# Causal attention and a gated FFN on one core: seven PSUM banks in one ring, exps per bank, and new orders of TensorE's work

## The chip, the cores and the metric

One core of a Trainium2 chip runs the kernel. The metric is device time in microseconds (us); the times before are three runs, and their median counts. Engines are called PE (TensorE), DVE (VectorE), ACT (ScalarE), POOL (GpSimd) and SP (SyncE, which only issues DMAs here).

## The reference

Eight batches `b` of 512 positions and 128 channels, 16 heads of width 8, then a gated FFN with a hidden width of 384; a LayerNorm (no gain, no bias) follows each.

```python
qkv = x @ w_qkv                                   # x (8, 512, 128), w_qkv (128, 384)
q, k, v = split(qkv, 3) -> (B, H=16, T=512, D=8)
att = einsum('bhtd,bhsd->bhts', q, k) / sqrt(D)
att = softmax(where(causal, att, -inf))
x = layernorm(x + einsum('bhts,bhsd->bhtd', att, v))
gate, up = x @ wg.T, x @ wu.T                     # int32 weights times 1/127
h = silu(gate) * up
x = layernorm(x + h @ wd.T)
```

All of it is float32.

## The kernel before, in words

**Groups.** The heads are worked on four at a time. A group `G` (0 to 31) is one quarter of the heads of one batch; a batch is four groups. q and k rows are split into a high and a low part (`parts`), written to DRAM scratch and read back in the layout that products need (`rows_of`, `read_rows`, `write_parts` on SP), two heads on each half of the rows: a head `hh` lies at row 64 * (hh % 2).

**Three passes over a group, at different times.**
1. *Maxima*, two groups ahead (`LAG = 2`): `maxima(M, k)` computes q against k with queries on the partitions, one PSUM bank for each k of 0 to 9 (`max_blocks`), two banks per call; DVE's `reduce_bank` takes minus the row maximum out of each block. Banks 0 to 3 hold 512 columns, the rest 384 + 128 or 256 + 256.
2. *Negated maxima*: POOL splits them in two parts (`split_negmax`); PE transposes them (`turn_negmax(m)`, one 128-column transpose); ACT copies them out of PSUM (`copy_negmax`, nm_T, L811); SP writes them into further rows of q (`load_negmax`, two DMAs of 8 KB, L347). `scores(m, 0)` waits for that with `pe.wait_ge(nm_loaded[G % 2], NM_LOADED * (G // 2 + 1))`.
3. *Scores and values*: `scores(G, s)` computes k against q with keys on the partitions, with the negated maximum as extra rows, into a pair of banks (slot `s`, 0 to 4); ACT's `exp_slot` applies exp to the pair at once (1024 columns, L803) into `pt`; POOL clears the part of the diagonal blocks above the diagonal (`clear_diagonal`, L1082); `values(V, piece)` multiplies with v for the group before (V = G - 1), in five pieces ("0a", "0b", "1", "2", "3": 256, 256, 384, 256, 128 columns; float32, which the trace shows as two matmuls for each), into bank 7, which stays outside of all rings. v carries a column of ones, so the row sums come along. Every two groups ACT copies the sum out (`copy_out`), PE transposes it (`turn_out`, four transposes) and DVE divides (`normalise`).

**PSUM.** Of eight banks, four form two pairs (`st_ps`) that scores, projections and x's transposes use in turn (`SCORE_TURNS`); three (`mx_ps`) are for maxima, negmax transposes and output transposes in turn (`MAXIMA_TURNS`). A turn waits until the turn that had its bank before has been read out (`pair_free`, `bank_free`).

**Order.** Every engine runs a list written out by hand. PE's is `group0` to `group3` (G % 4 of 1, 2, 3, 0). ACT's loop runs, for each group: exps of slots 0 and 1, `copy_negmax(G + 1)`, exps of slots 2 and 3, copies, slot 4. Projections for later batches: V and the turn of x in group0, Q and K in group1. `add_zeros(n)` adds n products of zeros to bank 7 and changes no value. `group0` before:

```python
scores(G, 0); scores(G, 1); later_values(V, "0a"); maxima(M, 0)
later_values(V, "1", "0b"); turn_negmax(G + 1); maxima(M, 2); scores(G, 2)
turn_out(half_of(G)); scores(G, 3); maxima(M, 4); later_values(V, "2", "3")
scores(G, 4); maxima(M, 6); project_v(b + 1); maxima(M, 8)
```

After the last group comes the FFN, batch by batch (`turn_x1`, `gate_up`, `down`), with both LayerNorms on DVE and POOL.

Of the kernel before, what the change touches and what calls it, by code (L numbers as in the profile page):

```python
# [40 lines left out]
SLOTS = 5  # L41
UNITS = 2 * SLOTS
# [40 lines left out]
def pieces_read(V, s):  # L83

    order = PIECE_ORDER[V % NG]
    return 1 + max(order.index(piece) for piece in (("0a", "0b"), ("0a", "0b"), ("1", "3"), ("1", "3"), ("2",))[s])


def score_turns():


    turns = [("X0",), ("QK",), ("VX", 0), ("Q", 1), ("K", 1), ("W", 0), ("W", 1)]
    for G in range(GROUPS):
        turns += [("S", G, s) for s in range(SLOTS - 1)]
        b, n = (G - 1) // NG, (G - 1) % NG
        if n == 1 and b + 2 < B:
            turns.append(("Q", b + 2))
        turns.append(("S", G, SLOTS - 1))
        if n == 0 and b + 1 < B:
            turns.append(("VX", b + 1))  # L100
        if n == 1 and b + 2 < B:
            turns.append(("K", b + 2))
    return turns


def maxima_turns():


    turns = []
    for G in range(-LAG, GROUPS + 1):  # L110
        n = (G - 1) % NG
        for k in range(MX):
            if G + LAG < GROUPS:
                turns.append(("M", G + LAG, k))
            if k == (1, 3, 3, 1)[n] and 0 <= G + 1 < GROUPS:
                turns.append(("N", G + 1))
            if k == (3, None, 5, None)[n] and G > 1:
                turns.append(("O", (G - 3) // 2))
    return turns + [("O", 2 * B - 1)]


SCORE_TURNS = score_turns()
MAXIMA_TURNS = maxima_turns()


def attention_ffn(nc, x, w_qkv, w_gate, w_up, w_down, out):
    ctx = ExitStack()
    with ctx:  # L128
# [7 lines left out]
        st_ps = [psum[:, 0:2, :], psum[:, 2:4, :]]  # L136
        mx_ps = [psum[:, 4, :], psum[:, 5, :], psum[:, 6, :]]
# [131 lines left out]
        def pair_of(*turn):  # L269
            return st_ps[SCORE_TURNS.index(turn) % 2]  # L270

        def pair_free(*turn):

            t = SCORE_TURNS.index(turn) - 2
            if t < 0:
                return []
            kind, *at = SCORE_TURNS[t]
            if kind == "X0":
                return [(xt_copied, 1)]
            if kind == "QK":  # L280
                return [(lo_made, 2)]
            if kind == "VX":
                return [(v_copied, at[0] + 1)] + ([(xt_copied, at[0] + 2)] if at[0] + 1 < B else [])
            if kind == "W":
                return [(wff_copied, 2 + at[0])]
            if kind == "S":
                return [(exp_done, SLOTS * at[0] + at[1] + 1)]
            return [(full_made, 2 * at[0] - (1 if kind == "Q" else 0))]

        def bank_of(*turn):  # L290
            return mx_ps[MAXIMA_TURNS.index(turn) % 3]

        def bank_free(*turn):

            t = MAXIMA_TURNS.index(turn) - 3
            if t < 0:
                return []
            kind, *at = MAXIMA_TURNS[t]
# [6 lines left out]
        def whole_batches(step):  # L305
            for b in range(B):
                step(b, b % 2, b == 0, b == B - 1)

        x1_ps = psum[:, 6, :]

        def y_ps(c):
            return psum[:, 4, :] if c < B - 1 else x1_ps

        last_pair = SCORE_TURNS.index(("S", GROUPS - 1, SLOTS - 2)) % 2
        ff_pairs = [(psum[:, 2 * p, :], psum[:, 2 * p + 1, :]) for p in (last_pair, 1 - last_pair)] + [(psum[:, 5, :], pv_ps)]
# [8 lines left out]
        def _(sp):  # L326
# [47 lines left out]
            for b in range(B):  # L374
                u = b % 2
                for n in range(NG):
                    if NG * b + n + 2 < GROUPS:
                        load_negmax(NG * b + n + 2)
                    if n == 0 and b < B - 1:
                        for g in (2, 3):  # L380
                            if b > 0:
                                sp.wait_ge(st_full, SLOTS * NG * b)
                            read_rows(b + 1, 1 - u, g)
# [11 lines left out]
                    if n == 3 and b + 2 < B:  # L395
                        sp.wait_ge(st_full, SLOTS * NG * b + SLOTS * 2)
                        for g in range(2):
                            read_rows(b + 2, u, g)
# [8 lines left out]
        def _(pe):  # L407
            def take_pair(*turn):
                for sem_, value in pair_free(*turn):
                    pe.wait_ge(sem_, value)  # L410
                return pair_of(*turn)

# [10 lines left out]
            def turn_x(b, dst):  # L423
                pe.wait_ge(x_in[b % 2], 16 * (b // 2) + 16)
                transposes4(dst, xa[b % 2][:].rearrange("p n c -> p (n c)")).then_inc(xt_made, 1)

            def project(b, n, dst):
                pe.wait_ge(xt_copied, b + 1)
                pe.matmul(dst, wqkv[:, C * n:C * n + C], xT[:], start=True, stop=True).then_inc((q_made, k_made)[n], 1)  # L429

            def project_q(b):
                if b < B:
                    project(b, 0, take_pair("Q", b)[:, 0, :])

            def project_k(b):
                if b < B:
                    project(b, 1, take_pair("K", b)[:, 0, :])

            def project_v(b):

                if b < B:
                    pair = take_pair("VX", b)
                    pe.wait_ge(xt_copied, b + 1)
                    for n in range(NB):
                        last = pe.matmul(pair[:, 0, C * n:C * n + C], xT[:, P * n:P * n + P], wqkv[:, 2 * C:3 * C],
                                         start=True, stop=True)
# [10 lines left out]
            def turn_out(hf):  # L457
                if hf is not None:
                    bank = take_bank("O", hf)
# [3 lines left out]
            def scores(G, s):  # L463
                u, g = G // NG % 2, G % NG
                if G < GROUPS:
                    if s == 0:
                        pe.wait_ge(nm_loaded[G % 2], NM_LOADED * (G // 2 + 1))
                    pair = take_pair("S", G, s)
                    for bank in (2 * s, 2 * s + 1):
                        blocks = [(hh, j) for hh in range(HG) for j in range(NB) if key_block_place(hh, j)[0] == bank]  # L470
                        for n, (hh, j) in enumerate(blocks):
                            col, width, at = key_block_place(hh, j)[1], T - P * j, 64 * (hh % 2)
                            last = pe.matmul(pair[:, bank % 2, col:col + width],  # L473
                                             kx[u][at:at + KS, 2 * g + hh // 2, P * j:P * j + P].bitcast(F32R),
                                             qx[u][at:at + KS, 2 * g + hh // 2, P * j:T].bitcast(F32R),
                                             start=(n == 0), stop=(n == len(blocks) - 1), skip_group_check=True)
                    last.then_inc(st_full, 1)

            def maxima(M, k):

                if M < GROUPS:
                    u, g = M // NG % 2, M % NG
                    if k == 0:
                        pe.wait_ge(qk_loaded[u][g], LOADED * (M // NG // 2 + 1))
                    for k in (k, k + 1):
# [50 lines left out]
            def group0(G):  # L536
                V, M, b = G - 1, G + LAG, G // NG
                scores(G, 0)
                scores(G, 1)
                later_values(V, "0a")  # L540
                maxima(M, 0)
                later_values(V, "1", "0b")
                if V == 0:
                    add_zeros(4)
                turn_negmax(G + 1)
                maxima(M, 2)
                scores(G, 2)
                turn_out(half_of(G))
                scores(G, 3)
                maxima(M, 4)  # L550
                later_values(V, "2", "3")
                scores(G, 4)
                maxima(M, 6)
                if b + 1 == B:
                    add_zeros(4)
                project_v(b + 1)
                maxima(M, 8)

            def group1(G):
                V, M, b = G - 1, G + LAG, G // NG  # L560
                values(V, "0a")
                scores(G, 0)
                scores(G, 1)
                maxima(M, 0)
                values(V, "1", "0b")
                maxima(M, 2)
                turn_negmax(G + 1)
                scores(G, 2)
                values(V, "2")
                maxima(M, 4)  # L570
                scores(G, 3)
                if b + 2 == B:
                    maxima(M, 6)
                    add_zeros(4)
                    scores(G, 4)
                    maxima(M, 8)
                    add_zeros(3)
                    values(V, "3")
                else:
                    values(V, "3")  # L580
                    maxima(M, 6)
                    project_q(b + 2)
                    scores(G, 4)
                    maxima(M, 8)
                    project_k(b + 2)

            def group2(G):
                V, M = G - 1, G + LAG
                maxima(M, 0)
                scores(G, 0)  # L590
                values(V, "0a")
# [611 lines left out]
```

## Time and profile before

| | |
|---|---|
| median of 3 runs | 353.14 us (351.8 to 357.61) |
| profiled execution, its own time | 353.12 us |
| its span | 351.4 us |
| PE busy | 333.8 us, 95% |
| DVE busy | 294.0 us, 84% |
| ACT busy | 214.7 us, 61% |
| POOL busy | 178.4 us, 51% |

The span is the time between the first and last record in the trace; the time has a little around it. Busy time counts an instruction from its start to its end, so overlapping matmuls on PE count once and a PE that is waiting with one in flight is busy. PEld is the loading of weights, which runs beside the matmuls.

### The profile page before, as it was taken

To read this page: it belongs to the slowest core of one execution; us is meant where nothing else is said; L and a number is where in the kernel's file an instruction comes from. 1 tells how busy PE (TensorE), PEld (TensorE's weight loads), DVE (VectorE), ACT (ScalarE), POOL (GpSimd) and SP (SyncE) were. 2 spreads that over 40 slices of the span, in tenths; PEclk is the share of its full clock that TensorE was granted. 3 is DMA by queue.
4 is the path that set the end of the run, shared out by engine and by line. 5 is a ranking of instruction groups with operands and counts; after the bars stand their busy time and mean duration, and the time that the engine had idled before them with its cause. 6 is when DMAs were issued, how large, how long until landed. Compare 5 with 4: busy or idle time off the path is not lost. (4 is left out here: it accounts for less than half of the span.)

```text
span 351.4 us, 9106 instructions
## 1 busy us (share of the span) xinstructions
PE 333.8 (95%) x2947; PEld 197.1 (56%) x2947; DVE 294.0 (84%) x1251; ACT 214.7 (61%) x277; POOL 178.4 (51%) x325
## 2 busy tenths in 40 slices
PE   7799999999999999999999999999999998999990
PEld 3444464556556555645564565456455544798980
DVE  7979778898899889889898998899898974867765
ACT  3402567777767768677777777776677784333320
POOL 8400334734654474357445534843434469787633
PEclk9999989999999999999999999999999999999997
DMA  5797242554265327624541653185100010002021
GB/s 155 288 296 250 62 123 64 197 171 123 62 245 174 109 73 261 168 73 169 198 121 34 245 147 110 41 288 165 49 2 5 5 34 1 3 30 62 30 62 60
DMA packets 33903, 41.75 MB, mean 119 GB/s; under 512 B 3136, under 2 KB 17472, under 8 KB 33856
## 3 DMA queue, kind: packets, MB, share of 16 engines
q1 hardware_dynamic: 33696, 40.91, 36.7%
q8 instruction: 24, 0.39, 0.5%
q10 hardware_dynamic: 160, 0.26, 0.2%
q14 instruction: 23, 0.19, 0.2%
HBM read 21.76 MB, written 18.87 MB: 116 GB/s over the span
## 5 line engine op out<-in xcount | busy, mean ns | idle before, releaser
L903 DVE CUSTOM_DVE_ANT_0 masked<-psum,mask 128x384 bf16<-128x384 f32 (+3 forms) x512 | 218.9, 487 | 30.7 <-PE psum L490 26.5
L803 ACT ACTIVATE pt<-psum 128x1024 f32<-128x1024 f32 x160 | 158.4, 1021 | 51.8 <-PE psum L473 51.2
L1082 POOL TENSOR_SCALAR_AFFINE_SELECT pt<-pt 128x512 f32<-128x512 f32 x128 | 79.6, 634 | 95.7 <-ACT pt L803 93.9
L490 PE MATMUL psum<-kx,qx 33*128 33x384 f32 (+3 forms) x512 | 91.8, 354 | 1.6 <-DVE nm L903 0.7
L513 PE MATMUL psum<-pt,vx 128*32 128x256 f32 (+2 forms) x1280 | 92.1, 388 | 1.1 <-ACT oT L817 0.8
L473 PE MATMUL psum<-qx,kx 35*128 35x384 f32 (+3 forms) x512 | 75.4, 342 | 0.5 <-ACT pt L803 0.5
L490 PEld LDWEIGHTS psum<-kx,qx 33*128 33x128 f32 x512 | 53.2, 186 | 37.8 <-DVE nm L903 18.6
L473 PEld LDWEIGHTS psum<-qx,kx 35*128 35x128 f32 x512 | 45.7, 185 | 29.0 <-issue 15.1
L513 PEld LDWEIGHTS psum<-pt,vx 128*32 128x32 f32 x1280 | 30.3, 109 | 38.3 <-issue 23.6
L903 DVE DVE_READ_ACCUMULATOR2_ANT nm<- 128x1 f32 x512 | 42.6, 83 | 0.0
L1070 POOL TENSOR_SCALAR nm_parts<-nm 128x16 fp32r<-128x16 f32 x32 | 6.6, 206 | 51.3 <-DVE nm L903 50.3
L867 ACT ACTIVATE sg<-psum 128x512 f32<-128x512 f32 x24 | 14.3, 598 | 27.6 <-PE psum L710 22.8
L811 ACT ACTIVATE nm_T<-psum 32x128 f32<-32x128 f32 x32 | 8.5, 266 | 26.1 <-PE psum L455 26.1
L723 PE MATMUL psum<-wT,pt 128*128 128x128 f32 x192 | 22.6, 275 | 0.0
L723 PEld LDWEIGHTS psum<-wT,pt 128*128 128x128 f32 x192 | 22.1, 192 | 0.1
L710 PE MATMUL psum<-x_lo,wT 128*128 128x512 f32 x48 | 19.2, 400 | 2.4 <-DVE x_lo L981 2.4
L708 PE MATMUL psum<-x_hi,wT 128*128 128x512 f32 x48 | 19.9, 415 | 0.0
L522 PE MATMUL psum<-zeros 128*128 128x512 bf16 x68 | 18.7, 406 | 1.2 <-DVE zeros L938 1.2
L993 DVE TENSOR_TENSOR pt<-psum,sg 128x512 f32<-128x512 f32 x24 | 15.8, 680 | 4.3 <-ACT sg L867 3.5
L429 PE MATMUL psum<-xT,wqkv 128*128 128x512 f32 x32 | 17.4, 636 | 0.1
L1101 POOL TENSOR_TENSOR parts<-full,parts 128x512 fp32r<-128x512 f32 x12 | 15.4, 1284 | 1.0
L1129 POOL TENSOR_TENSOR rstd<-veps,minus_half 128x4 f32<-128x4 f32 (+1 forms) x12 | 14.7, 1224 | 0.0
(64 smaller groups left out, 273.6 us busy)
## 6 DMA issues: line engine op xcount, KB each, us to landing
scr_q<-parts SPq DMA_DIRECT2D x16, 512.0 KB, 3.6
scr_k<-parts SPq DMA_DIRECT2D x16, 512.0 KB, 5.0
qx<-scr_q SPq DMA_DIRECT2D x64, 128.0 KB, 2.6
kx<-scr_k SPq DMA_DIRECT2D x62, 128.0 KB, 2.7
xa<-L_attn_x SPq DMA_DIRECT2D x8, 256.0 KB, 3.2
res<-L_attn_x SPq DMA_DIRECT2D x8, 256.0 KB, 2.8
out<-yo SPq DMA_DIRECT2D x8, 256.0 KB, 2.3
qx<-nm_T SPq DMA_DIRECT2D x64, 8.0 KB
```

Of the source, the lines that this page charges most:

```text
L429: pe.matmul(dst, wqkv[:, C * n:C * n + C], xT[:], start=True, stop=True).then_inc((q_made, k_made)[n], 1)
L473: last = pe.matmul(pair[:, bank % 2, col:col + width], kx[u][at:at + KS, 2 * g + hh // 2, P * j:P * j + P].bitcast(F32R), qx[u][at:at + KS ...
L490: last = pe.matmul(bank[:, col:col + width], qx[u][at:at + KM, 2 * g + hh // 2, P * i:P * i + P].bitcast(F32R), kx[u][at:at + KM, 2 * g + ...
L513: last = pe.matmul(pv_ps[VW * hh:VW * hh + VW, first:last_q], vx[u][:, at:at + VW], pt[g % 2][:, bank, col + first - P * j:col + last_q - ...
L522: pe.matmul(pv_ps, zeros[:, 0:P], zeros[:], start=True, stop=True, skip_group_check=True)
L708: pe.matmul(ff_ps(c, m)[n], w, x1_hi[c % 2][:].bitcast(F32R), start=True, stop=False)
L710: pe.matmul(ff_ps(c, m)[n], w, x1_lo[c % 2][:].bitcast(F32R), start=False, stop=True).then_inc(full, 1)
L723: last = pe.matmul(y_ps(c)[:, C * n:C * n + C], hid[c % 2][:, m, P * n:P * n + P], wT[:, 2, P * m:P * m + P], start=(m == 0 and n == 0), s ...
L803: act.activation(pt[G % 2][:, 2 * s:2 * s + 2, :], pair_of("S", G, s), ACT.Exp, scale=SM_SCALE).then_inc(exp_done, 1)
L903: dve.tensor_tensor_reduce(masked[count % 4][:, 0:width], bank[:, col:col + width], mask[:, T - width:T], -1.0, 3.0e38, ALU.add, ALU.min, ...
L993: dve.tensor_tensor(hid[c % 2][:, m, :], ff_ps(c, m)[1], sg[k % 2][:], ALU.mult).then_inc(hid_made, 1)
L1082: pool.affine_select(out=blocks, in_=blocks, pattern=[[0, HG], [1, P]], compare_op=ALU.is_ge, fill=0.0, base=0, channel_multiplier=-1).the ...
```

## The change

1. Both rings become one, `BANK_TURNS`, over seven banks (`RING = 7`): each turn, of whatever kind, takes the next bank and waits for the turn seven before it to be read out. The turn of x and the V projection, which shared a pair, are turns of their own.
2. Scores and exps go by banks: `scores(G, n)` for n of 0 to 9, and ACT's `exps` with 512 columns each instead of 1024.
3. `group0` to `group3` get new orders, with single banks of scores and maxima interleaved, and `turn_negmax` at other places; ACT's list puts `copy_negmax(G + 1)` behind exp 9 in group0 and group1, behind exp 3 in group2 and behind exp 8 in group3. DVE's `normalise` stands at other places.
4. Zero products: `project_v` adds four in the last batch, where there is nothing to project. Those of the first group (four) and of group1 in the batch before the last (four and three) go.
5. The FFN's banks get their numbers from the ring; `turn_out(2 * B - 1)` waits for the last exp.

```diff
-PIECE_ORDER = (("0a", "1", "0b", "2", "3"), ("0a", "1", "0b", "2", "3"), ("0a", "0b", "2", "3", "1"), ("0a", "0b", "1", "2", "3"))
+PIECE_ORDER = (("0a", "1", "0b", "3", "2"), ("0a", "1", "0b", "3", "2"), ("0a", "3", "2", "0b", "1"), ("0a", "0b", "1", "3", "2"))
...
+GROUP_TURNS = (
+    "s0 s1 m0 s2 s3 m1 m2 s4 m3 s5 m4 o n s6 m5 m6 s7 s8 s9 m7 m8 v x m9",
+    "m0 s0 s1 s2 s3 s4 m1 s5 m2 m3 m4 m5 s6 s7 m6 q s8 s9 m7 m8 n k m9",
+    "s0 s1 m0 m1 s2 m2 s3 n o s4 m3 s5 m4 m5 s6 m6 s7 m7 s8 m8 s9 m9",
+    "s0 s1 m0 s2 m1 s3 m2 s4 m3 s5 m4 n s6 m5 s7 s8 m6 m7 s9 m8 m9",
+)
...
+BANK_TURNS = bank_turns()
+RING = 7
...
+        def bank_of(*turn):
+            return psum[:, BANK_TURNS.index(turn) % RING, :]
+
+        def bank_free(*turn):
+
+            t = BANK_TURNS.index(turn) - RING
             if t < 0:
                 return []
...
+            if kind == "V":
+                return [(v_copied, at[0] + 1)]
             if kind == "W":
+                return [(wff_copied, at[0] + 1)]
             if kind == "S":
+                return [(exp_done, UNITS * at[0] + at[1] + 1)]
...
                     last.then_inc(v_made, 1)
-                    if b + 1 < B:
-                        turn_x(b + 1, pair[:, 1, :])
+                else:
+                    add_zeros(4)
...
             def group0(G):
                 V, M, b = G - 1, G + LAG, G // NG
+                scores(G, 0, 1)
                 maxima(M, 0)
+                later_values(V, "0a", "1")
+                scores(G, 2, 3)
+                maxima(M, 1, 2)
+                scores(G, 4)
+                maxima(M, 3)
+                later_values(V, "0b")
+                scores(G, 5)
+                maxima(M, 4)
+                turn_out(half_of(G))
                 turn_negmax(G + 1)
+                scores(G, 6)
+                maxima(M, 5, 6)
+                scores(G, 7)
+                later_values(V, "3", "2")
+                scores(G, 8, 9)
+                maxima(M, 7, 8)
                 project_v(b + 1)
+                turn_x(b + 2)
+                maxima(M, 9)
...
             def group1(G):
...
                 maxima(M, 0)
+                scores(G, 0, 1, 2, 3)
+                values(V, "0a", "1")
+                scores(G, 4)
+                maxima(M, 1)
+                scores(G, 5)
+                maxima(M, 2, 3, 4)
+                values(V, "0b", "3", "2")
+                maxima(M, 5)
+                scores(G, 6, 7)
+                maxima(M, 6)
+                project_q(b + 2)
+                scores(G, 8, 9)
+                maxima(M, 7, 8)
                 turn_negmax(G + 1)
+                project_k(b + 2)
+                maxima(M, 9)
...
             def group2(G):
...
+                scores(G, 0, 1)
+                maxima(M, 0, 1)
+                scores(G, 2)
+                values(V, "0a", "3")
                 maxima(M, 2)
+                scores(G, 3)
                 turn_negmax(G + 1)
                 turn_out(half_of(G))
+                scores(G, 4)
+                maxima(M, 3)
+                scores(G, 5)
+                maxima(M, 4, 5)
+                scores(G, 6)
+                values(V, "2")
                 maxima(M, 6)
+                scores(G, 7)
+                maxima(M, 7)
+                scores(G, 8)
+                values(V, "0b", "1")
                 maxima(M, 8)
+                scores(G, 9)
+                maxima(M, 9)
...
             def group3(G):
                 V, M = G - 1, G + LAG
                 scores(G, 0)
+                values(V, "0a")
+                scores(G, 1)
                 maxima(M, 0)
+                scores(G, 2)
+                maxima(M, 1)
+                values(V, "0b")
+                scores(G, 3)
                 maxima(M, 2)
+                scores(G, 4)
+                maxima(M, 3)
+                scores(G, 5)
                 maxima(M, 4)
                 values(V, "1")
+                turn_negmax(G + 1)
+                scores(G, 6)
+                maxima(M, 5)
+                scores(G, 7, 8)
+                maxima(M, 6, 7)
+                values(V, "3", "2")
+                scores(G, 9)
+                maxima(M, 8, 9)
...
-            turn_out(2 * B - 1)
+            pe.wait_ge(exp_done, UNITS * GROUPS)
+            turn_out(2 * B - 1, last_out)
...
+            def exps(G, *banks):
+                for n in banks:
+                    act.wait_ge(st_full, UNITS * G + n + 1)
                     if G > 1:
+                        act.wait_ge(pv_piece, PIECES * (G - 2) + pieces_read(G - 2, n))
+                    act.activation(pt[G % 2][:, n, :], bank_of("S", G, n), ACT.Exp, scale=SM_SCALE).then_inc(exp_done, 1)
...
+            for G in range(1, GROUPS - 1):
                 b, n = (G - 1) // NG, (G - 1) % NG
+                if n == 0:
+                    exps(G, 0, 1, 2, 3, 4, 5, 6, 7, 8, 9)
+                    copy_negmax(G + 1)
+                    copy_v_and_x(b + 1)
+                elif n == 1:
+                    exps(G, 0, 1, 2, 3, 4, 5, 6, 7)
+                    copy_q_or_k(b + 2, 0)
+                    exps(G, 8, 9)
+                    copy_negmax(G + 1)
                     copy_out((G - 2) // 2)
+                    copy_q_or_k(b + 2, 1)
+                elif n == 2:
+                    exps(G, 0, 1, 2, 3)
+                    copy_negmax(G + 1)
+                    exps(G, 4, 5, 6, 7, 8, 9)
+                else:
+                    exps(G, 0, 1, 2, 3, 4, 5, 6, 7, 8)
+                    copy_negmax(G + 1)
                     copy_out((G - 2) // 2)
+                    exps(G, 9)
...
-                    if k == (3, None, 5, None)[(G - 1) % NG] and half_of(G) is not None and G < GROUPS - 1:
+                    if k == (4, None, 2, None)[(G - 1) % NG] and half_of(G) is not None and G < GROUPS - 1:
                         normalise(half_of(G))
...
-                    pool.wait_ge(exp_done, SLOTS * G + s + 1)
+                    pool.wait_ge(exp_done, UNITS * G + (4, 8, 10, 8)[j])
```

## Rows read from the trace of the kernel before

**Rows 1.** The page, busy time of each engine.

```profile
PE 333.8 (95%) x2947; PEld 197.1 (56%) x2947; DVE 294.0 (84%) x1251; ACT 214.7 (61%) x277; POOL 178.4 (51%) x325
```

**Rows 2.** The waits: engine, line and tile, releaser, total us, times, longest.

```profile
PEld psum L490 <- DVE nm L903: 18.6, 59, 0.5
...
PEld psum L473 <- ACT pt L803: 12.1, 23, 0.8
...
PEld psum L473 <- DMA qx<-nm_T: 0.4, 1, 0.4
```

**Rows 3.** Busy time by stretch: PE, PEld, DVE, ACT, POOL, clock, DMA.

```profile
154.15:186.67 32.52, 32.35 (x318) 17.76 (x316) 28.79 (x133) 24.02 (x31) 16.56 (x29) 1.00 0.46 148
```

**Rows 4.** Timeline of PE: start us, us, line, tiles, shapes, count.

```profile
150.66 0.50 PE L490 MATMUL psum<-kx,qx 33*128 33x512 f32 x2
151.09 0.33 PE L455 MATMUL psum<-identf,nm_parts 128*128 128x128 f32 x1
151.35 0.50 PE L473 MATMUL psum<-qx,kx 35*128 35x384 f32 x4
151.78 0.64 PE L513 MATMUL psum<-pt,vx 128*32 128x256 f32 x8
152.35 0.65 PE L490 MATMUL psum<-kx,qx 33*128 33x384 f32 x3
...
154.15 1.13 PE L429 MATMUL psum<-xT,wqkv 128*128 128x512 f32 x2
155.20 0.51 PE L473 MATMUL psum<-qx,kx 35*128 35x256 f32 x4
...
163.65 0.51 PE L473 MATMUL psum<-qx,kx 35*128 35x256 f32 x4
...
165.91 0.42 PE L513 MATMUL psum<-pt,vx 128*32 128x256 f32 x4
...
177.85 0.51 PE L473 MATMUL psum<-qx,kx 35*128 35x256 f32 x4
...
178.53 1.16 PE L445 MATMUL psum<-wqkv,xT 128*128 128x128 f32 x8
179.52 0.60 PE L420 MATMUL psum<-identf,xa 128*128 128x128 f32 x4
180.05 0.51 PE L490 MATMUL psum<-kx,qx 33*128 33x256 f32 x4
```

**Rows 5.** Timeline of all engines around two negmax loads.

```profile
29.26 0.27 ACT L811 ACTIVATE nm_T<-psum 32x128 f32<-32x128 f32 x1 [13.52 <-PE psum L455]
...
29.55 1.52 SPq L347 DMA_DIRECT2D qx<-nm_T  x2
...
32.41 0.19 PEld L473 LDWEIGHTS psum<-qx,kx 35*128 35x128 f32 x2 [0.42 <-DMA qx<-nm_T]
...
160.07 0.33 PE L455 MATMUL psum<-identf,nm_parts 128*128 128x128 f32 x1
...
160.44 0.27 ACT L811 ACTIVATE nm_T<-psum 32x128 f32<-32x128 f32 x1 [0.24 <-PE psum L455]
...
160.73 1.27 SPq L347 DMA_DIRECT2D qx<-nm_T  x2
```

**Rows 6.** Timeline of ACT: 1024 columns twice, and 512 columns twice.

```profile
160.61 1.90 ACT L803 ACTIVATE pt<-psum 128x1024 f32<-128x1024 f32 x2
...
212.17 0.60 ACT L789 ACTIVATE vx<-psum 128x512 f32<-128x512 f32 x1 [0.29 <-PE psum L445]
212.67 0.59 ACT L770 ACTIVATE xT<-psum 128x512 f32<-128x512 f32 x1
```

**Rows 7.** Busy time by stretch, columns as in rows 3.

```profile
46.00:47.00 1.00, 0.55 (x6) 0.56 (x8) 1.00 (x5) 1.00 (x2) 0.00 (x0) 0.87 0.06 16
47.00:50.00 3.00, 3.00 (x18) 2.73 (x14) 1.81 (x12) 1.69 (x3) 1.81 (x3) 0.50 0.91 248
...
290.00:292.00 2.00, 1.24 (x17) 0.44 (x9) 1.74 (x10) 1.42 (x2) 2.00 (x5) 1.00 0.00 0
```

More of the change, by code:

```diff
@@ L89, in score_turns @@
[L89 to L103, printed above, removed]
@@ L106, in maxima_turns, with bank_turns @@
[L106 to L115, printed above, removed]
+    return 1 + max(order.index(piece) for piece in (("0a", "0b") if n < HG else ("1", "3") if n < 2 * HG else ("2",)))
+GROUP_TURNS = (
[4 rows of a table added]
+)
+def bank_turns():
+    turns = [("X", 0), ("Q", 0), ("K", 0), ("V", 0), ("X", 1), ("Q", 1), ("K", 1), ("W", 0), ("W", 1), ("W", 2)]
+    turns += [("M", 0, k) for k in range(MX)]
+    turns += [("M", 1, 0), ("M", 1, 1), ("M", 1, 2), ("M", 1, 3), ("N", 0)] + [("M", 1, k) for k in range(4, 8)]
+    turns += [("S", 0, 0), ("S", 0, 1), ("M", 1, 8), ("M", 1, 9), ("S", 0, 2), ("S", 0, 3), ("M", 2, 0), ("M", 2, 1), ("N", 1)]
+    turns += [("S", 0, 4), ("S", 0, 5), ("M", 2, 2), ("M", 2, 3), ("S", 0, 6), ("S", 0, 7), ("M", 2, 4), ("M", 2, 5)]
+    turns += [("S", 0, 8), ("S", 0, 9)] + [("M", 2, k) for k in range(6, 10)]
+    for G in range(1, GROUPS - 1):
+        b = (G - 1) // NG
+        for turn in GROUP_TURNS[(G - 1) % NG].split():
+            if turn[0] == "s":
+                turns.append(("S", G, int(turn[1])))
+            elif turn[0] == "m" and G + LAG < GROUPS:
+                turns.append(("M", G + LAG, int(turn[1])))
+            elif turn == "n":
@@ L116, in maxima_turns @@
                 turns.append(("N", G + 1))
-            if k == (3, None, 5, None)[n] and G > 1:
+            elif turn == "o" and G > 1:
                 turns.append(("O", (G - 3) // 2))
-    return turns + [("O", 2 * B - 1)]
-SCORE_TURNS = score_turns()
-MAXIMA_TURNS = maxima_turns()
+            elif turn in ("q", "k") and b + 2 < B:
+                turns.append((turn.upper(), b + 2))
+            elif turn == "v" and b + 1 < B:
+                turns.append(("V", b + 1))
+            elif turn == "x" and b + 2 < B:
+                turns.append(("X", b + 2))
@@ L126, in attention_ffn @@
+    G = GROUPS - 1
+    return turns + [("S", G, n) for n in range(8)] + [("X1",), ("S", G, 8), ("S", G, 9), ("O", 2 * B - 2)]
+BANK_TURNS = bank_turns()
+RING = 7
 def attention_ffn(nc, x, w_qkv, w_gate, w_up, w_down, out):
@@ L455, in turn_negmax, with turn_out, scores @@
                     pe.transpose(bank[:, 0:P], nm_parts[:], identf[:]).then_inc(nm_turned, 1)
-            def turn_out(hf):
+            def turn_out(hf, bank=None):
                 if hf is not None:
-                    bank = take_bank("O", hf)
+                    if bank is None:
+                        bank = take_bank("O", hf)
                     pe.wait_ge(ot_copied, hf + 1)
                     transposes4(bank, oT[:]).then_inc(o_turned, 1)
-            def scores(G, s):
+            def scores(G, *banks):
@@ L566, in group1 @@
-                maxima(M, 2)
-                turn_negmax(G + 1)
[L568 to L585, printed above, removed]
+                scores(G, 0, 1, 2, 3)
@@ L867, in silu @@
                 act.activation(sg[k % 2][:], ff_ps(c, m)[0], ACT.Silu, scale=W_SCALE).then_inc(silu_done, 1)
-            for s in range(SLOTS - 1):
-                exp_slot(GROUPS - 1, s)
-            exp_slot(GROUPS - 1, SLOTS - 1)
+            exps(GROUPS - 1, 0, 1, 2, 3, 4, 5, 6, 7, 8, 9)
             copy_x1(0)
```

283 lines of the change are left out of this document (100 added, 183 removed).

## The prediction

> **What bounds the kernel now.** Five views, in this order, the last two at the parts that need them. The profile's page gives TensorE (PE) 95% of the span and VectorE (DVE) 84% [rows 1], so PE is read first; but a busy PE is not a full one, because matmuls in flight count as busy. The chain of waits shows what PE's weight loads stood behind: DVE's readings of the maxima banks 18.6 us, ScalarE's (ACT's) exps 12.1 us, and the load of the negated maxima once, 0.4 us [rows 2]. A stretch of one batch (from one Q projection to the next, four groups) lasts 32.52 us, with DVE busy 28.79 and ACT 24.02 [rows 3]. The third view is PE's timeline, read from start to start [rows 4]. There, work falls into runs of one kind, and every change of kind costs something:
> - scores and maxima together: one step (two banks, one on each half of the rows, side by side) 150.66 to 151.09, 0.43 us; two steps 177.85 to 178.53, 0.68. So 0.25 a step and 0.18 for the change of kind.
> - values: 256 columns 151.78 to 152.35, 0.57; I split that as 0.13 for the change and 0.44 for the work, 0.22 per 128 columns.
> - transposes: one 151.09 to 151.35, 0.26; four 179.52 to 180.05, 0.53.
> - projections: Q or K 154.15 to 155.20, 1.05; V 178.53 to 179.52, 0.99.
>
> The loops have per batch 20 runs with 40 steps (20 x 0.18 + 40 x 0.25 = 13.6 us), 14 runs of values (14 x 0.13 + 4 x 2.2 = 10.6), 7 of transposes (2.7) and 3.1 of projections: 30.0 of 32.5 us. The other 2.5 us are stalls; the largest is plain: 163.65 to 165.91 is 2.26 us for four steps that need 1.18 [rows 4]. PE bounds the kernel; DVE, busy for 28.79, is the next, 3.7 us behind it.
>
> **Part 1, fewer changes of kind (a gain).** I counted the new orders. A batch has 17 runs of scores and maxima (saves 3 x 0.18), 12 of values (2 x 0.13) and the negmax and output transposes in one run twice (2 x 0.13): 1.1 us. Bank n of scores and bank k of maxima lie on the row half of their parity, and all single turns find a partner of the other half, so 40 steps remain; the singles cost nothing. PE's floor is 28.9 us a batch.
>
> **Part 2, one ring of seven.** The most that it can return is all stalls, 2.5 us a batch; the least is below nothing, since a score bank now also waits for DVE and a maxima bank for ACT. Taken with part 3, where a wait that is longer swallows both.
>
> **Part 3, the negated maxima come later (the loss).** Scores of group G+1 start only when three steps behind `turn_negmax(G+1)` are done: ACT's `copy_negmax`, two DMAs on SP, their landing. The one place in the trace where PE waited for the landing prices it: copy started at 29.26, PE's weight load at 32.41 after 0.42 us idle, 3.15 us. SP's two issues take 1.27 us in the steady part (160.73) and took 1.52 there, so I take 2.9 us from copy start to scores; the ends are 2.6 and 3.15. From transpose to copy it is 160.07 to 160.44, 0.37 us [rows 5]. Before, the transpose stands early in every group and ACT copies after two exp slots, so this is covered. The new orders take the cover away at three of four borders:
> - group1 to group2: the transpose is near the end. Behind it PE has K's projection, 1.05, and at most 0.2. Needed: 0.37 + 2.9 = 3.3. PE stands at least 1.9 us, whatever ACT does. ACT is later still: it copies after exps 8 and 9. Scores 8 and 9 come 5.85 us after the group's first (runs 0.67, 1.2, 0.9, 1.2, 0.76, 1.05); their data 0.4 later; Q's copy and two exps at 0.50 each (212.17 to 212.67 for 512 columns [rows 6]) put the copy at about 7.4, the next scores at 10.3.
> - group0 to group1: ACT copies only after exp 9. First scores to scores 8: 5.8 us (0.5, 1.2, 0.9, 0.57, 0.43, 0.7, 0.67, 0.79); data and two exps 1.4; copy at 7.2; next scores at 10.1. In the ring, maxima 7 takes the negmax bank of the same group, so part of that wait shows already there.
> - group3 to group0: ACT copies after exp 8. Scores 8 comes 4.4 us in (0.43, 0.57, 0.68, 0.57, 0.93, 0.79, 0.26, 0.2); with exps 6 to 8 in a row the copy starts at 6.2, the next scores at 9.1. PE has 1.7 us of work behind scores 8 and needs 3.9 or more.
> - group2 to group3: the transpose is early. PE's work is 6.4 us (0.8, 0.8, 0.43, 0.7, 0.9, 0.57, 0.68, 1.2, 0.3); DVE's share of a group is 7.2 (28.79 / 4), of which the ring lets some spill into the next, so 6.6.
>
> Sum: 10.1 + 10.3 + 6.6 + 9.1 = 36.1 us a batch, against 32.5: +3.6. In seven batches 25 us, the two borders of the last batch 3.5 more (2.4 and 1.2, the second shorter since no maxima are left), less 2.6 for eleven zero products that go (seven in the batch before the last, four in the first group), each priced as a step of 512 columns: +26 us.
>
> Who stands behind the waits: on PE everything, since its order is fixed, so DVE runs dry after at most three or four reductions, and ACT and POOL with it. On SP the load is issued ahead of `read_rows` and `write_parts` as before; these shift with it and are needed a group or more later, so I charge nothing for them. If that cover were gone, a group's maxima would wait for rows, some 2.6 us a time.
>
> **Part 4, exps per bank.** Two of 1024 columns take 1.90 us together, one of 512 takes 0.50 to the next [rows 6]: 4.6 us a group become 5.0, 1.6 us a batch on an engine with 8.5 us free. It starts PE's bank turns sooner, and sits on the chain above only with its last one to three exps. POOL's diagonal clearing waits for the same data as before: nothing. The last stage, behind group 31, gets other bank numbers for the same products in the same order, with one more wait, for the last exp, ahead of the last `turn_out`; the projections of the gate and up weights cover it: nothing.
>
> **Part 5, the clock.** PE's granted clock fell once in mid-kernel: PE was busy for 0.55 of the microsecond 46 to 47, with scores and maxima alone (clock 0.87), then ran at 0.50, which is 1.2 of 2.4 GHz, in 47 to 50 [rows 7]. That is 0.26 + 3.0 us at half speed at the least, and half of it is lost: 1.6 us a fall. In 290 to 292 PE was busy for only 1.24 of 2 us beside dense products, and the clock held. The new stalls are of 1.9 to 2.3 us, between runs of scores. Some will make it fall; I take 9 of 23 borders, 1.6 us each, 14 us; the ends are none and 23 (37 us). The Trainium skill, page "TensorE: Matmul & The Clock Gate", section "A second HAM failure mode: psum-queue depth-cycling", says that a TensorE that idles briefly between groups of matmuls, while it cycles through PSUM banks, can swing between the two levels. Taken as a rule for every border it would give the upper end; the stretch at 290 us does not bear that out.
>
> **The sum.** Profiled before: span 351.4, time 353.12, equal to the median 353.14. 353 + 26 + 14 = 393 us.
>
> **The rivals.**
> 1. The waits bind and the clock holds throughout: 353 + 26 = 379 us; with 2.6 us for the load it is 7 less (0.3 at 22 borders), 372. For it: 290 to 292. Against: the fall in 46 to 47 us after far less idling.
> 2. The waits bind and the clock falls at most borders: 353 + 26 + 37 = 416. For it: that fall. Against: the stall of 163.65 to 165.91, also among scores and maxima, and no fall.
> 3. Faster: the load isn't late. Then the stalls of part 2 go and PE comes near its floor, with DVE (28.79 busy) as next bound: 29.8 us a batch would be 353 - 7.25 x 2.7 = 333 (2.7 is 32.5 less 29.8). It decides if copy to scores takes under about 0.8 us instead of 2.9 (6.3 us a batch less, over three borders). For it: only 0.4 us of waiting on that load in the trace [rows 2]. Against: 160.73 plus 1.27 of issuing alone is 1.56 us behind the copy's start [rows 5].
> 4. It changes nothing: the load is late, but the late transposes gain what they lose because PE would have stood for DVE anyway. At most the 2.5 us of stalls a batch and the 1.1 of part 1 can pay; that takes 1.2 us less at each of the three borders, a load of 1.7 us. About 353.
>
> **How the numbers follow.** Forecast (some falls) 0.46, rival 1 0.27, rival 2 0.10, rival 3 0.10, rival 4 0.07. Predicted 393. The range leaves out rivals 3 and 4 and the far end of 2: 364 (rival 1 with a load of 2.6, less 8 for what the runs of PE overlap better than priced) to 422 (rival 2 with a load of 3.15). A measurement here tells about 2% from no change, 7 us. Faster 0.10, same 0.07, slower 0.83.
>
> **What the profile after would show.** Right: PE or its weight loads waiting for the load of the negated maxima some 22 times, 1 to 2.3 us each, where it was 0.4 us in all; batches of some 36 to 38 us; DVE under 80%; several slices with a clock below 0.9; fewer changes of kind. Wrong if: those waits are short, since ACT or the DMAs are quicker than priced; or PE waits for DVE or ACT in the ring instead; or DVE is above 90% (rival 3). Forecast and rivals 1 and 2 are told apart by the granted clock alone.

## The result: 501 us, and the profile after

The changed kernel takes 500.95 us (median of 4 runs, 493.7 to 506.1) against 353.45 us: 1.40 times as long (95% interval 1.393 to 1.416). The ratio and its interval compare only runs within 1.5% of the fastest of their kernel, while the medians, here and below, are of all runs. The forecast was 393 us with a range of 364 to 422. The direction and the late load of the negated maxima were right; the price put on a fall of the clock was not, and the size was not even near.

The profiled execution's page, with its span, the busy times that answer to [rows 1], and the slices (busy tenths in 40 equal slices of the span, and PE's granted clock in tenths):

```profile
span 491.9 us, 9391 instructions
PE 442.4 (90%) x2936; PEld 255.6 (52%) x2936; DVE 297.4 (60%) x1251; ACT 225.9 (46%) x437; POOL 179.0 (36%) x325
...
PE   8898899998889999889889999889987988889993
...
PEclk9999955585755555585755555765557655799998
```

DVE does the same work as before (297.4 us, 294.0 before) in a span 140 us longer, so it is no bound. PE's busy time rose from 333.8 to 442.4 us with eleven matmuls fewer. Only the clock row explains that: from the sixth slice to the 34th it reads mostly 5, which is 1.2 GHz of 2.4. The mean over the span is 0.684; if every microsecond was at one of the two levels, 63% of the span was at the lower.

The chain of waits, with the rows that answer to [rows 2]:

```profile
PEld psum L464 <- DMA qx<-nm_T: 26.9, 16, 2.7
...
PE psum L464 <- DMA qx<-nm_T: 21.0, 14, 2.5
...
PEld psum L464 <- DVE nm L902: 20.2, 29, 1.5
...
PEld psum L480 <- ACT nm_T L807: 12.5, 8, 1.6
...
PEld psum L464 <- ACT pt L800: 11.2, 17, 0.8
```

The load of the negated maxima, 0.4 us in all before, now holds PE 16 times for 26.9 us; and eight times a maxima bank waits for ACT's copy of them, which is maxima 7 of group0 taking the negmax bank of its own group. The order of the wait can be read at one border, group1 to group2 (timeline of all engines):

```profile
163.42 0.47 PE L446 MATMUL psum<-identf,nm_parts 128*128 128x128 f32 x1
163.69 1.92 PE L420 MATMUL psum<-xT,wqkv 128*128 128x512 f32 x2
164.06 0.25 ACT L807 ACTIVATE nm_T<-psum 32x128 f32<-32x128 f32 x1
164.34 1.28 SPq L340 DMA_DIRECT2D qx<-nm_T  x2
166.97 0.29 PEld L464 LDWEIGHTS psum<-qx,kx 35*128 35x128 f32 x2 [0.93 <-DMA qx<-nm_T]
```

From copy to scores: 164.06 to 166.97, 2.91 us, where 2.9 was taken. The transpose stands last in the group, as the diff has it. But PE waits for only 0.93 us here, not for 1.9 or more, because K's projection behind the transpose runs at half speed. At a border that PE reaches at the full clock it stands longer: 2.17 us ahead of the scores at 61.56 us. Busy time by stretch (PE, PEld, DVE, ACT, POOL, clock, DMA), as in [rows 3] and [rows 7]:

```profile
48.00:51.00 3.00, 3.00 (x17) 2.61 (x14) 1.47 (x8) 0.60 (x1) 0.34 (x1) 0.50 0.39 103
51.00:61.00 10.00, 8.39 (x79) 4.51 (x79) 7.62 (x36) 7.40 (x15) 3.42 (x9) 0.99 0.27 78
61.00:102.00 41.00, 38.26 (x236) 21.59 (x237) 21.88 (x96) 17.73 (x35) 12.01 (x20) 0.51 0.29 97
102.00:112.00 10.00, 8.84 (x82) 4.66 (x80) 7.62 (x36) 7.75 (x16) 4.25 (x8) 0.98 0.30 88
...
133.00:208.00 75.00, 68.87 (x403) 38.36 (x403) 37.66 (x168) 32.12 (x63) 20.20 (x36) 0.50 0.26 81
```

The first fall, at 48 us, lasts 3 us, like the one in the kernel before. The next lasts 41 us, a later one 75. In all there are nine such stretches behind the first: 41, 13, 75, 14, 75, 44, 14, 24 and 3 us, some 304 us together. Eight of them begin beside a wait for the load, the last beside a wait of 2.20 us for one of ACT's copies. Matmuls pass at 8 a microsecond at the full clock (79 in 10 us) and 5.4 at the lower (403 in 75). One batch inside such a stretch, from V projection to V projection, takes 57 us against 32.5; V's projection itself 1.87 us (148.28 to 150.15) against 0.99 [rows 4]:

```profile
148.45:205.49 57.04, 53.95 (x317) 29.31 (x318) 29.56 (x133) 25.82 (x50) 16.63 (x29) 0.50 0.27 85
```

```profile
148.28 2.08 PE L436 MATMUL psum<-wqkv,xT 128*128 128x128 f32 x8
150.15 1.06 PE L408 MATMUL psum<-identf,xa 128*128 128x128 f32 x4
```

What stood ahead of the rises is mixed. The clock came back at the end of V's projection and x's transposes near 51, 102, 208 and 314 us, and behind values near 126, 232 and 389. It did not come back behind the V projection and transposes shown here, nor behind those at 254 us.

### The profile page after: what moved, and what is told of

Read it like the earlier page. It is cut to its first block and busy times, and to the rows that moved or that the text cites. A ratio compares the mean times of both kernels' runs of the same rounds, so it can differ in the third digit from the quotient of the medians.

```text
span 491.9 us, 9391 instructions
## 1 busy us (share of the span) xinstructions
PE 442.4 (90%) x2936; PEld 255.6 (52%) x2936; DVE 297.4 (60%) x1251; ACT 225.9 (46%) x437; POOL 179.0 (36%) x325
## 5 line engine op out<-in xcount | busy, mean ns | idle before, releaser
L800 ACT ACTIVATE pt<-psum 128x512 f32<-128x512 f32 x320 | 172.6, 598 | 172.8 <-PE psum L464 171.3
L464 PE MATMUL psum<-qx,kx 35*128 35x384 f32 (+3 forms) x512 | 145.6, 473 | 23.1 <-DMA qx<-nm_T 21.0
L480 PE MATMUL psum<-kx,qx 33*128 33x384 f32 (+3 forms) x512 | 145.6, 459 | 10.4 <-ACT nm_T L807 10.2
L503 PE MATMUL psum<-pt,vx 128*32 128x256 f32 (+2 forms) x1280 | 137.0, 558 | 2.7 <-ACT oT L813 2.2
L464 PEld LDWEIGHTS psum<-qx,kx 35*128 35x128 f32 x512 | 92.0, 271 | 89.0 <-DMA qx<-nm_T 26.9
L480 PEld LDWEIGHTS psum<-kx,qx 33*128 33x128 f32 x512 | 95.2, 268 | 48.1 <-issue 30.0
L503 PEld LDWEIGHTS psum<-pt,vx 128*32 128x32 f32 x1280 | 40.0, 140 | 49.8 <-issue 41.7
L420 PE MATMUL psum<-xT,wqkv 128*128 128x512 f32 x32 | 21.1, 757 | 0.0
L408 PE MATMUL psum<-identf,oT 128*128 128x128 f32 x64 | 16.4, 407 | 0.0
L436 PE MATMUL psum<-wqkv,xT 128*128 128x128 f32 x64 | 15.6, 420 | 0.0
```

The source lines that it names most:

```text
L408: last = pe.transpose(dst[:, P * n:P * n + P], src[:, P * n:P * n + P], identf[:])
L420: pe.matmul(bank, wqkv[:, C * n:C * n + C], xT[:], start=True, stop=True).then_inc((q_made, k_made)[n], 1)
L464: last = pe.matmul(bank[:, col:col + width], kx[u][at:at + KS, 2 * g + hh // 2, P * j:P * j + P].bitcast(F32R), qx[u][at:at + KS, 2 * g + ...
L480: last = pe.matmul(bank[:, col:col + width], qx[u][at:at + KM, 2 * g + hh // 2, P * i:P * i + P].bitcast(F32R), kx[u][at:at + KM, 2 * g + ...
L503: last = pe.matmul(pv_ps[VW * hh:VW * hh + VW, first:last_q], vx[u][:, at:at + VW], pt[g % 2][:, bank, col + first - P * j:col + last_q - ...
L800: act.activation(pt[G % 2][:, n, :], bank_of("S", G, n), ACT.Exp, scale=SM_SCALE).then_inc(exp_done, 1)
```

## The experiments

Two theories stood. Mine: the late negated maxima make PE stand at three of four borders, and standing lets the clock fall. The rival: the ring, the single exps or the new orders cost by themselves, in waits or through the clock.

### 1. The change with the negmax early

The ring, the exps of 512 and all orders stay; only the transpose and the copy move forward. In the ring's lists, in PE's functions and in ACT's loop alike:

```diff
-    "... m3 s5 m4 o n s6 ..."           # group0, ACT copies behind exp 9
+    "... m3 n s5 m4 o s6 ..."           # behind exp 4
-    "... m4 m5 ... s8 s9 m7 m8 n k m9"  # group1, behind exp 9
+    "... m4 n m5 ... s8 s9 m7 m8 k m9"  # behind exp 5
-                values(V, "1")          # group3, behind exp 8
                 turn_negmax(G + 1)
+                values(V, "1")          # behind exp 4
```

> The changed kernel with its ring, exps and orders, but the negmax transpose and ACT's copy of it early in every group (transposes ahead of scores 5 in group0, behind the values in the middle of group1, ahead of values 1 in group3; the copy behind exps 4, 5, 3 and 4). My theory (late negated maxima make PE stand at the group borders, and the standing keeps the clock down): waits for the negmax load under 3 us in all, clock over 0.95, DVE over 85% busy, 330 to 350 us. Rival (the ring and the new orders cost by themselves): waits for that load gone but the time over 370 us, with PE waiting for DVE or ACT at banks of the ring.

Measured: 344.32 us (340.1 to 348.8), 0.963 of the kernel before (0.955 to 0.971), mean clock 0.952. One batch, and the waits for the load:

```profile
137.83:167.75 29.92, 29.92 (x320) 17.82 (x316) 28.14 (x134) 24.85 (x51) 16.52 (x30) 1.00 0.50 162
```

```profile
PEld psum L464 <- DMA qx<-nm_T: 2.0, 2, 1.2
```

The rival falls: with everything else of the change in place, a batch takes 29.92 us against 32.52 [rows 3], and the whole kernel is faster than before. Moving one 128-column transpose and one copy, in three groups of every four, is worth 157 us. What still holds this version back shows behind the place where group1 of the batch before the last has no projections any more:

```profile
229.00:233.60 4.60, 4.60 (x57) 2.47 (x55) 3.63 (x15) 3.65 (x7) 2.73 (x5) 1.00 0.49 148
233.60:237.90 4.30, 3.29 (x28) 2.33 (x32) 4.30 (x27) 3.41 (x8) 1.81 (x3) 1.00 0.22 65
237.90:248.00 10.10, 10.10 (x73) 5.78 (x65) 6.22 (x28) 4.53 (x10) 2.28 (x5) 0.51 0.01 2
```

PE was busy for 3.29 of 4.30 us, with scores and maxima alone and DVE as the bound. Then the clock was at 0.51 for 10 us, though PE was never idle in them.

### 2. The kernel before with the negmax late

Pairs, three banks, exps of 1024 and the old orders; only the transpose and the copy move back to where the change has them, as near as pairs allow (in group3 the copy stands behind the last exp and not one ahead of it).

```diff
-            if k == (1, 3, 3, 1)[n] and 0 <= G + 1 < GROUPS:
+            if k == ((1, 3, 3, 1) if G < 1 else (5, 9, 3, 5))[n] and 0 <= G + 1 < GROUPS:
...
                 exp_slot(G, 1)
-                copy_negmax(G + 1)
+                if n == 2 or G < 1:
+                    copy_negmax(G + 1)
...
                 exp_slot(G, 4)
+                if n != 2 and G > 0:
+                    copy_negmax(G + 1)
```

(and `turn_negmax` in `group0`, `group1` and `group3` to match)

> The kernel before with its pairs, its three banks and its exps of 1024, but the negmax transpose and copy where the change has them (transpose behind maxima 4 in group0, behind the last maxima in group1, behind values 1 in group3; the copy behind the last exps there). My theory: the late load alone makes it slow, 430 to 510 us, with over 30 us of waits for the load and a mean clock of 0.65 to 0.8. Rival (the ring and orders do it): under 375 us, clock over 0.95.

Measured: 450.18 us (442.8 to 459.6), mean clock 0.831, waits for the load 40.4 us in 21 places:

```profile
PEld psum L473 <- DMA qx<-nm_T: 40.4, 21, 2.7
```

```profile
139.05:185.70 46.65, 42.17 (x318) 22.42 (x318) 29.22 (x133) 23.78 (x31) 16.61 (x29) 0.76 0.32 104
```

So the late load is also enough by itself, with no ring: 96 us between the medians, 91 between the fastest runs (442.8 and 351.7). The clock is down for less of the time than forecast (0.831, and 0.805 to 0.843 over the four runs; I expected at most 0.8).

### 3. The change, with zero products in place of idling

```diff
                     bank = take_bank("S", G, n)
                     if n == 0:
+                        for _ in range((0, 8, 4, 8)[G % NG] if G > 1 else 0):
+                            pe.matmul(bank, zeros[:, 0:P], zeros[:], start=True, stop=True, skip_group_check=True)
                         pe.wait_ge(nm_loaded[G % 2], NM_LOADED * (G // 2 + 1))
```

> The changed kernel as it is, with eight products of zeros (four ahead of group2's neighbour group1) written to the bank of scores 0 while PE would stand for the negmax load: about 1.8 us of dense work in the place of idling; scores 0 then overwrites the bank. My theory (the waits cost some 3.6 us a batch at full clock, all the rest is the clock, and idling at the borders is what keeps it down): clock over 0.95, 370 to 390 us, as priced in my first rival. Rival (the clock is down because of the order of the work within the groups): clock under 0.8 still, over 450 us.

Measured: 397.9 us (397.7 to 408.5), ratio 1.126 (1.119 to 1.134). Adding 152 matmuls made the changed kernel 103 us faster, and the rival (the order within the groups, over 450 us) falls. The profiled execution took 408.5 us at a mean clock of 0.935. From 91 to 255 us it ran at the full clock; a batch there gives what the change costs without the clock's part, with 20 zero products in it:

```profile
164.65:201.97 37.32, 35.47 (x339) 19.68 (x338) 28.66 (x133) 24.91 (x50) 16.66 (x29) 1.00 0.40 130
```

37.3 us a batch, against 36.1 worked out for the change. The forecast of 370 to 390 was still too low by 8 us. The mean clock of 0.964 to 0.966 in the three other runs leaves room for that, but no run parts it out. The zeros do two things at once: PE no longer idles, and the work in that place covers the whole array (128 rows by 128 columns). No run here tells which of the two holds the clock.

### 4. Only ACT's copy early

```diff
-                    exps(G, 0, 1, 2, 3, 4, 5, 6, 7, 8, 9)
-                    copy_negmax(G + 1)
+                    exps(G, 0, 1, 2, 3, 4, 5)             # group0; in group3 likewise behind exp 5
+                    copy_negmax(G + 1)
+                    exps(G, 6, 7, 8, 9)
```

> The changed kernel, only ACT's copy of the negated maxima as soon as PE's order has the transpose done (behind exp 5 in group0, exp 5 in group3, behind exp 9 in group1 as before). PE's order isn't touched. My theory: borders group0/group1 and group3/group0 lose 2 and 1 us of waiting, group1/group2 keeps 2; 355 us if one wait a batch lets the clock be, 380 to 430 if it doesn't. Rival (ACT's place of the copy is harmless, PE's order decides): within 10 us of the changed kernel.

Measured: 395.0, 402.2, 448.0 and 452.7 us, median 425. Two of four runs lie in the forecast range of 380 to 430 and two above. All four are over 40 us below the changed kernel's lowest, so ACT's place of the copy is not harmless and the rival falls. The same program differs by 57 us from run to run, where the other versions spread over 2 to 17 us and that of experiment 8 over 30. The mean clock differs with it: 0.867 and 0.846 at 395 and 402 us, 0.731 and 0.722 at 448 and 453. Nothing here shows why.

### 5. The early version with zeros where projections are missing

```diff
                 project_q(b + 2)
+                if b + 2 >= B:
+                    fill(4, "S", G, 8)      # four zero products in that turn's bank
                 scores(G, 8, 9)
...
                 project_k(b + 2)
+                if b + 2 == B:
+                    fill(4, "M", M, 9)
+                elif b + 1 == B:
+                    fill(4, "S", G + 1, 0)
```

> The early-negmax version of the change, plus four zero products (of about 0.24 us each) at each of the four places in the last two batches where group1 has no Q or K to project, written to a bank that the next turn overwrites. In that version's trace the clock is down for 10.2 us from 237.9 and for 13.7 us from 268.6 us, both behind those places. My theory (idling among scores and maxima lets the clock fall, and it stays down while the work is sparse): both stretches go, half of 24 us is won and at most 4 us paid: 332 to 338 us, every profile's mean clock over 0.97. Rival (the falls come with DVE and ACT as the bound there, zeros only add): 344 us or more.

Measured: 335.44 us (333.6 to 338.1), ratio 0.950 (0.946 to 0.954). As forecast; both late stretches at the lower clock are gone. The profiled execution (338.1 us, mean 0.976) has an early one instead, 11 us from 47 us on, with PE busy in all of it; the other five runs have mean clocks of 0.984 to 0.993. This is the fastest version of the study: 5% below the kernel before.

### 6. Ten more in the first group

```diff
                 later_values(V, "0a", "1")
+                if V == 0:
+                    add_zeros(4)            # and 3 behind "0b", 3 behind "3", "2"
```

> The same, and ten more zero products in the first group, at the places of the values that it doesn't have. In the kernel before and in all others the clock is down for 3.4 us from about 47 us. Theory: they take the place of idling (0.5 to 1 us), cost up to 1.4 us and give back 1.7: within 1 us of the version without them. Rival: PE has nothing to spare there, 2 us slower.

Measured: 336.98 us (334.9 to 337.2), ratio 0.951 (0.948 to 0.955). The difference from the version without them, 1.5 us, is not clear of noise. The mean clocks are not apart either (0.986 to 0.995, against 0.976 to 0.993), and in this trace the clock is down for 3 us from 35 us on in place of 47. So the zeros there bought nothing that these runs show.

### 7. One late border

The early version of experiment 1, with group1's transpose and copy at the end of the group again.

> The early-negmax version with one border put back: group1's transpose and copy stand at the end of the group, as in the change. One wait of about 2.3 us a batch (seven batches). At full clock that is 344 + 16 = 360 us. If a single wait a batch is enough to let the clock fall and keep it down, 380 to 430 us with a mean clock under 0.85; if the clock needs several waits to fall, 355 to 365 us and over 0.93. I expect the first by six to four, since the clock fell in the early version too, behind two sparse places.

Measured: 408.65 us (399.2 to 413.5), mean clock 0.825. One wait a batch costs 64 us between the medians, 59 between the fastest runs. By stretch, the waits below:

```profile
58.00:72.00 14.00, 13.25 (x88) 7.28 (x90) 7.35 (x33) 6.15 (x12) 6.00 (x9) 0.52 0.54 191
72.00:99.00 27.00, 24.83 (x256) 14.66 (x257) 22.99 (x107) 20.63 (x43) 12.66 (x24) 1.00 0.35 101
99.00:133.00 34.00, 34.00 (x216) 19.59 (x216) 20.08 (x92) 16.75 (x33) 10.23 (x18) 0.50 0.40 126
```

```profile
PEld psum L464 <- DMA qx<-nm_T: 18.5, 9, 2.7
```

In 99 to 133 us PE was busy for all of 34 us, and the clock stayed at 0.50 throughout. So in this stretch it was not idling that held the lower level. PE did scores and maxima on 33 or 35 of 128 rows, values and a few transposes, and the clock came back only at 132.6 us, at the end of V's projection and x's transposes. Nor does the work alone set the length: the same order stands behind this border in every batch but the last ones, PE waits 2.15 to 2.51 us at it seven times, a fall goes with each wait, and the falls last 14, 34, 27, 10, 10, 13 and 13 us. What decides between 10 and 34 stays open.

### 8. A ring of six banks

```diff
-RING = 7
+RING = 6
```

(with bank 6 left alone for the ring's last output transpose)

> The early-negmax version with a ring of six banks (the last output transpose keeps the seventh). If the width of the ring is what makes this version faster than the kernel before (fewer stalls at banks), a ring of six costs 5 us or more: 350 to 365 us. If it is the fewer changes of kind and the new orders, it stays within 3 us of 344.

Measured: 362.58 us (352.8 to 382.9), mean clock 0.949. A batch at the full clock:

```profile
146.87:178.97 32.10, 31.81 (x317) 18.55 (x318) 28.49 (x133) 25.08 (x51) 16.61 (x30) 1.00 0.47 151
```

32.10 us against 29.92 with seven banks, so the width is worth 2.2 us a batch, or 16 us of the kernel, and without it all the rest of the change together gives 0.4 us a batch over the kernel before. The profiled executions bear that out: 359.25 us at a mean clock of 0.949 against 344.32 at 0.952, 15 us apart with the clock alike. The medians are 18 us apart, the fastest runs 13.

### 9 and 10. The late border filled, and its control

The 335 us version; in experiment 9 with group1's negmax late as in experiment 7, in both with eight zero products ahead of the scores of group2.

```diff
                     if n == 0:
+                        for _ in range(8 if G > 1 and G % NG == 3 else 0):
+                            pe.matmul(bank, zeros[:, 0:P], zeros[:], start=True, stop=True, skip_group_check=True)
                         pe.wait_ge(nm_loaded[G % 2], NM_LOADED * (G // 2 + 1))
```

> The 335 us version with group1's negmax late again (one wait a batch, which made 344 into 409 us), but PE does eight zero products (some 1.9 us) in the bank of scores 0 while it waits. The wait stays as long as it was; only the idling goes. If the clock is what a late wait costs: a mean clock over 0.95 and 335 + 7 x 2.5 = 350 to 358 us. If it is the wait itself, or what stands behind it, over 380 us.

> The 335 us version with the same eight zero products ahead of group2, and the negmax early, so that they fill no wait: the control. PE is the bound there, so seven times 1.9 us, less what they hide of stalls (up to 0.8 us a batch): 343 to 349 us, clock over 0.96. If the zeros should be cheap because PE has spare time at the border: under 340.

Measured: 354.7 us (353.7 to 362.9) with the late border, ratio 1.005 (1.000 to 1.010), and 354.09 us (350.7 to 357.1) for the control. The border in experiment 9, and a batch of each:

```profile
124.66 1.90 PE L466 MATMUL psum<-zeros 128*128 128x512 bf16 x8
126.86 0.50 PE L471 MATMUL psum<-qx,kx 35*128 35x512 f32 x2 [0.31 <-DMA qx<-nm_T]
```

```profile
147.30:179.60 32.30, 32.01 (x325) 18.60 (x326) 28.40 (x133) 24.85 (x51) 16.61 (x30) 1.00 0.46 152
```

```profile
144.68:176.77 32.09, 32.09 (x326) 18.61 (x326) 28.39 (x133) 25.01 (x51) 16.62 (x31) 1.00 0.46 151
```

The load is as late as in experiment 7. PE works 1.90 us and then still waits 0.31. The late border costs 32.3 - 29.9 = 2.4 us a batch here, and the kernel 19 us (354.7 against 335.4). In experiment 7, idle, it cost 64 us (408.7 against 344.3). So some 45 of those 64 us, or 39 of 59 between the fastest runs, came through the clock. Experiment 9 came out as forecast (350 to 358 us, a clock above 0.95; it was 0.983). The control misses its forecast by 5 to 11 us: eight zero products cost 2.15 us a batch, a little more than their 1.90, and hid no stalls. With the zeros in both, the late border differs from the early one by 0.2 us a batch and by nothing that the two kernel times can tell apart.

## Why the prediction was wrong, point by point

**What bounds the kernel.** Right. PE with DVE behind it; with the load early and the new orders a batch comes to 29.92 us, where part 1's floor was 28.9.

**Part 1, changes of kind.** A saving of 1.1 us a batch was counted. It was not tested alone. Experiment 8 has it together with the new orders and the single exps in a ring of six: 0.4 us a batch for all of them.

**Part 2, the ring.** Taken as swallowed by part 3, and bounded by 2.5 us a batch. With the load early, ring, orders and fewer changes of kind give 2.6 us a batch together, and of that the seventh bank gives 2.2 (experiment 8).

**Part 3, the late load.** Right, and measured at 2.91 us from copy to scores against 2.9 (2.9 also at 58.66 to 61.56 us). A batch at the full clock was put at 36.1 us; with experiment 3's zeros in it, it is 37.3. That is 4.8 us above the kernel before and 7.4 above the early version. PE's standing at the border group1 to group2 was put at 1.9 us or more; at the full clock it is 2.17 us. Undoing this alone makes the kernel faster than before (experiment 1), doing it alone makes the old one over 90 us slower (experiment 2). Rival 3, whose condition was a load under 0.8 us, was rightly held to be unlikely.

**Part 4, exps per bank.** ACT's busy time rose from 24.02 us a batch [rows 3] to 24.85 in the early version, where 1.6 was the estimate; with PE and DVE busy for longer in both.

**Part 5, the clock: the step that failed.** "Some will make it fall; I take 9 of 23 borders, 1.6 us each, 14 us; the ends are none and 23 (37 us)." The mistake is the price of a fall, not how many there are: the trace has nine of them behind the first, as many as taken, though that the count came out is luck, since nothing in the working named the borders. The price was taken from the one fall in the trace of before, which ended after 3.4 us under V's projection and the transposes of x, and I read that length as belonging to every fall. In the changed kernel the nine last 3 to 75 us, 34 on average; at a mean clock of 0.684, some 310 us of the span lie at half speed, where the upper end of my range had 75. Put together: the change at the full clock costs 37.3 - 32.5 = 4.8 us a batch, 35 us in all (with the zeros of experiment 3 in it), and the other 112 of the 147 us are the clock. What fails is the form of the term, a number of falls times a fixed length. A batch that lies wholly at the lower clock takes 57.0 us against 37.3, so about a third of the time spent there is lost; a third of some 304 us is 105, near the 112.

The Trainium skill, page "TensorE: Matmul & The Clock Gate", section "A second HAM failure mode: psum-queue depth-cycling", tells of a TensorE that idles briefly between groups of matmuls and swings between the two levels, and it pointed to rival 2. This trace agrees, with ten falls in mid-kernel and a mean clock of 0.684. But rival 2 priced every border with the same 1.6 us and came to 416. What ends a fall stays open: V's projection stood ahead of some rises and not of others, and one order of work ended falls after 10 us and after 34 (experiment 7).

**What the profile was to show.** DVE under 80% (60%), the waits (16 of some 22, up to 2.7 us), fewer changes of kind and slices below 0.9: all there. Batches of 36 to 38 us: none seen in the changed kernel, whose batches inside the long stretches take 57 us; 37.3 in experiment 3, where the clock held. That the clock would tell forecast and rivals apart was right.

## What to carry to other kernels

A load behind a chain (a transpose, a copy on a busy engine and two DMAs, here 2.9 us from copy to scores) belongs early in the order, even where its result is wanted late: in experiment 7 seven idle gaps of 2.15 to 2.51 us cost about 60 us. The length of one fall of PE's clock is no price for the next: here it was 3 us in the kernel before and up to 75 in the changed one, so price the share of time that may lie at the lower level, and give a range that holds the long case. Where PE must wait, zero products into a bank that the next turn overwrites are a cheap guard: eight of them, 1.90 us, cost 2.15 us where there was no wait, and saved some 45 us of the kernel where there was one.

## What the runs showed of the hardware that was not expected

- A clock of 0.50 outlasts full business: 34.0 of 34.0 us busy in experiment 7 before it rose, and 10.1 of 10.1 us in experiment 1.
- Behind one and the same order of work, with 2.15 to 2.51 us of idling ahead, the lower level lasted 10 to 34 us (experiment 7).
- The version with only ACT's copy early ran in 395 to 453 us, with mean clocks of 0.867 down to 0.722. Where the clock held throughout a batch, its length repeated to 0.1 us (29.92 and 29.94 in two kernels).
- 152 matmuls more made a kernel 103 us faster.
